# Third and fifth layer of an eight-layer kernel: output transposes and output projection of a group moved to the next round of the loop

## The chip, the cores and the metric

The kernel runs on one core of a Trainium2 chip. The metric is the device time of one execution in microseconds (us), compared by the median over runs. The engines are PE (TensorE; PEld are its weight loads), DVE (VectorE), ACT (ScalarE), POOL (GpSimd) and SP (SyncE, which here only issues DMAs). Each engine works through its own instructions in the order in which the program gives them, and waits at semaphores for the others.

## The reference

Eight residual layers are applied to x, of shape 128 sequences by 64 tokens by 128 features, in float32. Odd layers (first, third, fifth, seventh) are cross-attention to `ctx`; even ones are feed-forward layers. Only the third and the fifth are rearranged by the change:

```python
# third layer, "l1x": 16 heads of 8 features
q = (LN(x) @ Wq.T + bq) * scale;  k = ctx @ Wk.T + bk;  v = ctx @ Wv.T + bv
probs = softmax(q k^T + mask);    x = x + tanh(g) * ((probs v) @ Wo.T + bo)
# fifth layer, "l2x": 4 query heads of 32 features, one key/value head, rotary positions
q = rope(rms(LN(x)) @ q_w);  k = rope(rms(ctx) @ k_w);  v = rms(ctx) @ v_w
x = x + tanh(g) * (softmax(mask(q k^T)) v @ out_w)
```

## The kernel before, in words

x stays in SBUF for the whole kernel. Each layer walks over 32 groups of 256 tokens (four sequences; two tiles, t = 0 and 1, of 128 tokens). A layer is software-pipelined: `make_layers` (L126 to L150) gives it a string of items, and every engine passes the same string once per round (`traverse`, L491 to L521). A word's suffix is its lag against the round: `+` is the group after the round's own, `++` two after, `-` the group before, `--` two before. Each engine has its own `do`, which issues only what that engine has to do for an item, and nothing where it has no part. So an item's place in the string is its place in the queue of every engine that takes part in it.

```python
last = min(lag for _, lag in layer.order)
first = 1 if last >= -1 else 3
for i in range(-2, first):  iteration(...)           # written out
count = (NG - 2 - first) // 2                        # loop of two rounds each
for i in range(first + 2 * count, NG - last):        # written out
```

The items of the third and fifth layer, with the lines of their instructions:

- L: statistics of x (and of ctx in the fifth), nine to fifteen short DVE instructions (L1417 to L1450), then a power on POOL (L745) and on SP one DMA of the group's ctx (L595, L588).
- M: normalisation on DVE (L1458, L1462). F: transposes of the result on PE (L821, L825), copied out by ACT (L1200, L1194).
- QK (third): the query and key products on PE (L844 to L845), copied out by ACT (L1210, L1212), after which SP spreads the keys over the heads with 16 DMAs (L602). Q, K (fifth): products on PE, rotary arithmetic on DVE (L1619 to L1629). V: products on PE, copied out by ACT (L1225, L1233).
- S0, S1: scores of a tile on PE; then, in the same item, the DVE part of the softmax: mask, maximum, difference (L1540, L1543, L1545). In the third layer S0 waits on PE for all key-spreading DMAs of its group. P0, P1: the exponentials on ACT (L1260).
- T0, T1: transposes of the probabilities on PE (L942), copied out by ACT (L1266). The third layer has eight chunks, so each T takes two PSUM banks; the fifth has two chunks and takes one.
- A0, A1: probabilities times values on PE, then on DVE the reciprocal of the sums and the scaling into `o_sb` (L1663, L1667).
- X0, X1: transposes of `o_sb` on PE (L974), copied into `oT` by ACT (L1281, L1284). They wait until DVE has written `o_sb`.
- W0, W1: output projection on PE (L994); then on DVE, in the third layer, the bias (L1703) and the residual (L1578), in the fifth the residual alone. The last reader frees the PSUM bank: L1703 in the third layer, L1578 in the fifth.

T, A, X and W of one group share two PSUM banks, 6 and 7, in turn (`body_ring`): in the third layer T0 takes 6 and 7, T1 takes 6 and 7, A0 6, A1 7, X0 6, X1 7, W0 6, W1 7; in the fifth T0 6, T1 7, A0 6, A1 7, X0 6, X1 7, W0 6, W1 7. F, Q, K, V take banks 4 and 5, and the scores banks 0 to 3. Before PE writes a bank it waits until the bank's earlier content was read:

```python
def take(ring, g, u):                                    # L767
    b = ring.bank(g, u)
    pe.wait_ge(drained[b], ring.count(g, u) - 1)
    return b
```

The order of a ring's uses comes from the order of the string (L104 to L107).

Of the kernel before, what the change touches and what calls it, by code (L numbers as in the profile page):

```python
# [86 lines left out]
class Layer:  # L87
# [8 lines left out]
    def __init__(self, n, name, order, uses, body_banks, heads=0, scale=1.0, cross=False,  # L96
                 experts=0, top=0):
        self.n, self.name, self.order, self.uses = n, name, order, uses
        self.body_banks = body_banks
        self.heads, self.scale, self.cross = heads, scale, cross  # L100
        self.experts, self.top = experts, top
        self.front = []
        self.body = []
        for item, lag in order:  # L104
            if item[0] in ("L", "M", "H", "S", "P", "N"):
                continue
            (self.front if lag == 1 else self.body).extend([item] * uses.get(item[0], 1))  # L107
# [6 lines left out]
def stages(text):  # L114

    out = []
    for word in text.split():
        name = word.rstrip("+-")
        lag = word.count("+") - word.count("-")
        kind = name.rstrip("0123456789.")  # L120
        numbers = [int(k) for k in name[len(kind):].split(".")] if name != kind else [0]
        out.append(((kind, *numbers), lag))
    return out


def make_layers():  # L126
    attention = {"T": 2, "A": 2}
    narrow = {"T": 2, "A": 1}
    l0x = Layer(0, "l0x", stages(
        "L++ T0- S0 T1- S1 P0 F+ A0- M++ Q0+ N0 K0+ A1- N1 Q1+ P1 Q2+ W0- Q3+ W1- V0+"),  # L130
        attention, (6, 7), 16, 64 ** -0.5, True)
    l0f = Layer(1, "l0f", stages(
        "T1- S0 F+ T0- QK+ L++ G+ S1 A0- P0 H+ P1 E0.0+ E0.1+ A1- C+ V0+ N0 N1 Z0+ E1.0+ E1.1+ M++ Z1+"),
        narrow, (6, 7), 16, 8 ** -0.5, False, E_FF0, 2)
    l1x = Layer(2, "l1x", stages(
        "F+ S0 QK+ S1 L++ T0- T1- N0 A0- A1- P0 P1 N1 M++ V+ X0- X1- W0- W1-"),
        narrow, (6, 7), 16, 8 ** -0.5, True)
    l1f = Layer(3, "l1f", stages(
        "U0.0 U0.1 U0.2 L++ U1.0 U1.1 F+ D0 U1.2 U2.0 U2.1 U2.2 D1 U3.0 U3.1 D2 U3.2 "
        "U4.0 U4.1 U4.2 M++ D3 G+ D4 U5.0 U5.1 U5.2 H+ U6.0 U6.1 U6.2 D5 U7.0 U7.1 U7.2 "  # L140
        "D6 D7"), {}, (0, 1, 2, 3), experts=E_FF1, top=2)
    l2x = Layer(4, "l2x", stages(
        "S0 L++ F+ S1 Q+ T0- T1- P0 A0- P1 A1- K+ N0 M++ X0- X1- N1 W0- V+ W1-"),
        {"T": 1, "A": 1}, (6, 7), 4, 32 ** -0.5, True)
    l2f = Layer(5, "l2f", [], {}, (0, 1, 2, 3), experts=E_FF2, top=1)
    l3x = Layer(6, "l3x", stages(
        "T0- S0 T1- F+ P0 S1 Q2+ N0 Q0+ A0- K2+ P1 Q1+ A1- V2+ N1 K0+ W0- Q3+ K3+ L++ V0+ W1- M++ V3+ K1+ V1+"),
        attention, (6, 7), 16, 64 ** -0.5, True)
    l3f = Layer(7, "l3f", stages("KF L++ F+ M++ RF VF"), {}, (0, 1, 2))
    return [l0x, l0f, l1x, l1f, l2x, l2f, l3x, l3f]  # L150
# [73 lines left out]

def build(nc, x_in, ctx_in, ctxT_in, mask1_in, mask2_in, small_in, late_in, w1_in, w2_in, out):
    layers = make_layers()
    L0X, L0F, L1X, L1F, L2X, L2F, L3X, L3F = layers

# [1811 lines left out]
```

## Time and profile before

| | us |
|---|---|
| median of 3 runs | 4499.69 |
| lowest, highest | 4495.56, 4502.85 |
| the profiled execution, its own time | 4495.28 |
| its span, first to last instruction | 4493.3 |
| granted TensorE clock, mean over the span | 0.863 |

The rows further down are read like this. A row of the timeline is the start (us from the span's start), the length of a run of like instructions, the engine, the line and the operation, the tiles written and read, the count, and in brackets the engine's idle time just ahead and what ended it. In a row of stretches the columns are the stretch, its length, then for each engine its busy time with the count of instructions, the granted TensorE clock (1.00 is 2.4 GHz, 0.50 is 1.2 GHz), the DMA share and GB/s. The third layer runs from about 1374 to 1924 us, the fifth from about 2887 to 3262 us.

### The profile page before, as it was taken

To read this page: it belongs to the slowest core of one execution; us is meant where nothing else is said; L and a number is where in the kernel's file an instruction comes from. 1 tells how busy PE (TensorE), PEld (TensorE's weight loads), DVE (VectorE), ACT (ScalarE), POOL (GpSimd) and SP (SyncE) were. 2 spreads that over 40 slices of the span, in tenths; PEclk is the share of its full clock that TensorE was granted. 3 is DMA by queue.
4 is the path that set the end of the run, shared out by engine and by line. 5 is a ranking of instruction groups with operands and counts; after the bars stand their busy time and mean duration, and the time that the engine had idled before them with its cause. 6 is when DMAs were issued, how large, how long until landed. Compare 5 with 4: busy or idle time off the path is not lost.

```text
span 4493.3 us, 111186 instructions
## 1 busy us (share of the span) xinstructions
PE 3848.1 (86%) x38938; PEld 3008.1 (67%) x38938; DVE 2983.7 (66%) x9018; ACT 1953.3 (43%) x5436; POOL 884.4 (20%) x639
## 2 busy tenths in 40 slices
PE   5999978888886888889999999877845899999965
PEld 4777745555554556589999999755545767777754
DVE  4666657777765777766666666699972266666669
ACT  3666645655552434333333333222212355555521
POOL 1222223333330000010111111100062032222211
PEclk9999977777776767789999999988757999999976
DMA  3000010000001000000000000100004400000000
GB/s 130 8 7 8 7 23 6 6 6 6 6 7 68 15 16 15 14 6 0 0 0 0 0 0 3 43 11 11 8 22 166 147 13 12 12 12 12 10 13 26
DMA packets 102378, 98.15 MB, mean 22 GB/s; under 512 B 31728, under 2 KB 91120, under 8 KB 101616
## 3 DMA queue, kind: packets, MB, share of 16 engines
q1 hardware_dynamic: 97728, 77.99, 5.8%
q0 software_dynamic: 4096, 8.40, 0.6%
q10 hardware_dynamic: 432, 10.19, 0.6%
q8 instruction: 70, 1.15, 0.1%
q14 instruction: 52, 0.43, 0.0%
HBM read 48.02 MB, written 19.66 MB: 15 GB/s over the span
## 4 chain that ended last, share of the span: by engine, by line
PE 56%; DVE 20%; SPq 8%; issue 8%; POOL 3%; DMA 2%; ACT 2%; DVEq 1%; POOLq 0%; ACTq 0%
PE ps L781 52%; SPq L602 7%; PE ps L942 4%; DVE acc L1685 2%; DMA arena_a<-kT 1%; POOL route L753 1%; POOL scr L731 1%; DVE mx L1554 1%; DVE probs L1556 1%; DVE arena_b L1627 1%; DVE st L1417 1%; DVE o_sb L1667 1%; DVE xn L1458 1%; DVE vsmall L1635 1%; DVE mx L1543 1%
## 5 line engine op out<-in xcount | busy, mean ns | idle before, releaser
L781 PE MATMUL ps<-xcT,small 128*128 128x256 f32 x2176 | 618.4, 422 | 54.1 <-DMA xcT<-in_ctxT 27.2
L781 PEld LDWEIGHTS ps<-xcT,small 128*128 128x128 f32 x2176 | 412.4, 204 | 266.9 <-issue 105.5
L1294 ACT ACTIVATE kT<-ps 128x256 f32<-128x256 f32 (+1 forms) x768 | 294.4, 383 | 625.2 <-PE ps L781 549.0
L781 PE MATMUL ps<-arena_b,qT 64*64 64x64 f32 (+3 forms) x11136 | 543.6, 242 | 21.8 <-DVE arena_b L1627 20.4
L745 POOL TENSOR_TENSOR rstd<-veps,neghalf 128x2 f32<-128x2 f32 (+1 forms) x224 | 167.6, 748 | 1959.5 <-DVE veps L1450 1626.1
L759 POOL TENSOR_TENSOR probs<-probs,den 128x1024 f32<-128x1024 f32 x192 | 363.6, 1901 | 936.7 <-DVE den L1574 669.7
L781 PE MATMUL ps<-xhi,parts_a 128*128 128x256 f32 (+1 forms) x2112 | 501.2, 289 | 22.7 <-DVE qT L1714 22.7
L781 PE MATMUL ps<-small,xcT 128*64 128x64 f32 (+5 forms) x3072 | 482.1, 383 | 44.9 <-DVE acc L1685 33.1
L781 PEld LDWEIGHTS ps<-arena_b,qT 64*64 64x64 f32 (+3 forms) x11136 | 463.6, 149 | 59.1 <-issue 36.4
L1266 ACT ACTIVATE pT<-ps 128x512 f32<-128x512 f32 (+1 forms) x576 | 302.1, 571 | 435.6 <-PE ps L942 434.6
L1714 DVE TENSOR_TENSOR qT<-kT,ps 128x256 f32<-128x256 f32 (+1 forms) x768 | 316.5, 419 | 191.3 <-ACT kT L1294 184.0
L781 PE MATMUL ps<-xlo,parts_a 128*128 128x256 f32 (+1 forms) x1536 | 431.0, 281 | 0.0
L781 PEld LDWEIGHTS ps<-xhi,parts_a 128*128 128x128 f32 (+1 forms) x2112 | 350.1, 181 | 28.9 <-DVE qT L1714 28.0
L781 PE MATMUL ps<-small,oT 128*64 128x128 f32 (+1 forms) x2304 | 331.4, 295 | 22.4 <-ACT oT L1281 16.8
L942 PE MATMUL ps<-small,probs 128*128 128x128 f32 x2176 | 326.9, 296 | 17.4 <-ACT pT L1266 8.2
L781 PEld LDWEIGHTS ps<-small,oT 128*64 128x64 f32 (+1 forms) x2304 | 283.8, 155 | 83.3 <-issue 47.0
L942 PEld LDWEIGHTS ps<-small,probs 128*128 128x128 f32 x2176 | 262.6, 152 | 113.3 <-issue 81.5
L781 PEld LDWEIGHTS ps<-small,xcT 128*64 128x64 f32 (+1 forms) x3072 | 230.9, 180 | 154.5 <-DVE acc L1685 45.7
L781 PEld LDWEIGHTS ps<-vsmall,pT 128*128 128x128 f32 x2304 | 278.6, 197 | 71.6 <-issue 42.4
L781 PE MATMUL ps<-arena_a,qT 64*64 64x512 f32 (+1 forms) x1648 | 273.0, 633 | 45.9 <-DMA arena_a<-kT 45.9
L1274 ACT ACTIVATE oT<-ps 64x512 f32<-64x512 f32 x512 | 288.5, 587 | 48.5 <-PE ps L781 45.5
L1248 ACT ACTIVATE probs<-ps,negmax 128x64 f32<-128x64 f32 x1024 | 303.8, 418 | 0.0
(217 smaller groups left out, 7133.3 us busy)
## 6 DMA issues: line engine op xcount, KB each, us to landing
wbuf<-parts_b SPq DMA_DIRECT2D x39, 512.0 KB, 3.0
arena_a<-kT SPq DMA_DIRECT2D x1024, 8.0 KB
xcT<-in_ctxT SPq DMA_DIRECT2D x96, 128.0 KB, 2.1
xn<-scr SPq DMA_DIRECT2D x39, 128.0 KB, 2.2
scr_y<-acc SPq DMA_DIRECT2D x39, 128.0 KB, 2.9
scr<-vsmall SPq DMA_DIRECT2D x9, 512.0 KB, 13.4
ctx_sb<-in_ctx SPq DMA_DIRECT2D x32, 128.0 KB, 2.1
arena_a<-in_w ACTq DMA_DIRECT2D x1, 4096.0 KB, 12.1
```

The lines of the kernel that those rows point to most:

```text
L602: sp.dma_start(k_spread(g.par)[8 * h:8 * h + 8, h, :], kT[8 * h:8 * h + 8, g.par, :]).then_inc(s_kspread.sem(g), 16)
L731: pool.indirect_dma_start(out=scr[:, :], out_offset=bass.IndirectOffsetOnAxis(ap=place[:, t:t + 1], axis=0), in_=xn_all[:, t, :], in_offse ...
L745: pool.tensor_tensor(rstd[:, 0:n], veps[:, 0:n], neghalf[:, 0:n], ALU.pow).then_inc(s_rstd.sem, 1)
L759: pool.tensor_tensor(pr, pr, rv[:, t, 0:nh].unsqueeze(2).to_broadcast([P, nh, S]), ALU.mult).then_inc(s_probs.sem, 1)
L781: return nc.tensor.matmul(o, lhsT, rhs, start=start, stop=stop, skip_group_check=True)
L942: last = nc.tensor.transpose(bank(b)[:, i * P:(i + 1) * P], probs[:, g.par, t, c * P:(c + 1) * P], ident)
L1248: last = nc.scalar.activation(probs[:, g.par, t, h * S:(h + 1) * S], score_bank(b)[:, h * S:(h + 1) * S], ACT.Exp, bias=negmax[:, t, h:h + ...
L1266: nc.scalar.activation(pT[:, t, 4 * j:4 * j + n, :].rearrange("p c t -> p (c t)"), bank(b, n * P), ACT.Copy).then_inc(drained[b], 1)
L1274: last = nc.scalar.activation(oT[rows, t, :, hb * S:(hb + 1) * S], bank(b)[rows, :].rearrange("p (c q) -> p c q", q=S), ACT.Copy)
L1294: nc.scalar.activation(silu_buf(k)[0:n, :], bank(b)[0:n, 0:GT], ACT.Silu).then_inc(s_act.sem, 1)
L1685: add = dve.scalar_tensor_tensor(out=a, in0=src, scalar=cw, in1=a, op0=ALU.mult, op1=ALU.add)
L1714: dve.tensor_tensor(qT[0:n, e % 2, c, :], silu_buf(k)[0:n, :], bank(b)[0:n, GT:2 * GT], ALU.mult).then_inc(drained[b], 1)
```

## The change

In the third layer X0, X1, W0 and W1, which stood at the end of the round for the group before the round's own, now stand near its beginning for the group two before: it is the same group, reached one round later. X0 and X1 are put between F and S0, W0 between QK and S1, and W1 behind L. In the fifth layer X0 and X1 are put behind S0, and W0 and W1 behind F, ahead of S1. The sort in `Layer.__init__` only sees to it that the uses of banks 6 and 7 keep their order T, A, X, W. As the smallest lag is now -2, these two layers write out five rounds ahead of the loop in place of three and go one round further at the end.

```diff
-        for item, lag in order:
+        for item, lag in sorted(order, key=lambda e: -min(e[1], 0)):
...
     l1x = Layer(2, "l1x", stages(
-        "F+ S0 QK+ S1 L++ T0- T1- N0 A0- A1- P0 P1 N1 M++ V+ X0- X1- W0- W1-"),
+        "F+ X0-- X1-- S0 QK+ W0-- S1 L++ W1-- T0- T1- N0 A0- A1- P0 P1 N1 M++ V+"),
...
     l2x = Layer(4, "l2x", stages(
-        "S0 L++ F+ S1 Q+ T0- T1- P0 A0- P1 A1- K+ N0 M++ X0- X1- N1 W0- V+ W1-"),
+        "S0 X0-- X1-- L++ F+ W0-- W1-- S1 Q+ T0- T1- P0 A0- P1 A1- K+ N0 M++ N1 V+"),
```

## Rows read from the trace of the kernel before

**Rows 1.** Source view of L1545 in the third, then in the fifth layer (one per tile)
```profile
L1545 DVE TENSOR_TENSOR probs<-probs,mx x64: 1224/1224/1227, 1379.0 to 1907.1; 128x1024 f32<-128x1024 f32 x64
...
L1545 DVE TENSOR_TENSOR probs<-probs,mx x64: 424/424/426, 2895.7 to 3254.0; 128x256 f32<-128x256 f32 x64
```

**Rows 2.** Stretches: the steady part of the third layer, then of the fifth
```profile
1417.00:1900.00 483.00, 424.71 (x2635) 278.89 (x2638) 346.68 (x796) 193.19 (x370) 19.49 (x28) 0.70 0.06 16
2890.00:3250.00 360.00, 285.44 (x1676) 185.59 (x1674) 337.83 (x1254) 97.91 (x277) 30.20 (x30) 0.80 0.04 11
```

**Rows 3.** Chain that ended last, third layer, 1600 to 1634 us: start, length, what
```profile
1599.70 0.67 SPq L602
...
1609.09 0.62 SPq L602
...
1609.75 1.81 DMA arena_a<-kT
1611.56 0.14 issue
1611.69 4.00 PE ps L781 x12
```

**Rows 4.** Timeline of the third layer, one round and the start of the next
```profile
1611.69 1.99 PE L781 MATMUL ps<-arena_a,qT 64*64 64x512 f32 x8 [1.03 <-DMA arena_a<-kT]
...
1614.00 1.22 DVE L1540 SCALAR_TENSOR_TENSOR probs<-masked,ps 128x1024 f32<-128x1024 f32 x1 [2.63 <-PE ps L781]
...
1616.51 1.22 DVE L1545 TENSOR_TENSOR probs<-probs,mx 128x1024 f32<-128x1024 f32 x1
1616.59 10.67 SPq L602 DMA_DIRECT2D arena_a<-kT  x16
...
1617.53 1.14 PE L942 MATMUL ps<-small,probs 128*128 128x128 f32 x8
1617.94 1.22 DVE L1540 SCALAR_TENSOR_TENSOR probs<-masked,ps 128x1024 f32<-128x1024 f32 x1 [0.21 <-issue]
...
1620.26 3.76 PE L781 MATMUL ps<-vsmall,pT 128*128 128x36 f32 x32 [0.20 <-ACT pT L1266]
...
1621.60 0.48 DVE L1417 BATCH_NORM_STATS2 st<-x_sb 128x6 f32 x2
...
1623.07 0.36 DVE L1663 RECIPROCAL den<-ps 128x32 f32<-128x32 f32 x1
...
1625.10 0.60 DVE L1458 TENSOR_SCALAR xn<-x_sb,mv,rstd 128x128 f32 x2
...
1626.80 0.29 DVE L1703 TENSOR_TENSOR acc<-ps,small 128x128 f32<-128x128 f32 x1 [1.10 <-PE ps L781]
...
1626.98 0.63 PE L821 MATMUL ps<-small,xn 128*128 128x128 f32 x2
1627.26 0.35 DVE L1578 SCALAR_TENSOR_TENSOR x_sb<-acc,tgate,x_sb 128x128 f32 x1 [0.17 <-DVE acc L1703]
```

**Rows 5.** Stretches of that round, third layer: transposes to values, then the rest
```profile
1617.60:1624.30 6.70, 6.25 (x60) 5.66 (x62) 6.24 (x18) 4.18 (x6) 0.69 (x1) 1.00 0.05 12
1624.50:1633.40 8.90, 7.45 (x31) 3.42 (x28) 4.78 (x10) 2.50 (x7) 0.00 (x0) 0.50 0.07 20
```

**Rows 6.** Timeline of the third layer's last transposes and value products
```profile
1912.11 3.26 PE L942 MATMUL ps<-small,probs 128*128 128x128 f32 x16
...
1915.63 4.82 PE L781 MATMUL ps<-vsmall,pT 128*128 128x36 f32 x32 [0.26 <-issue]
```

**Rows 7.** Stretches beside rows 6: clock while transposing, then in the values' first half
```profile
1911.30:1914.60 3.30, 3.05 (x13) 2.78 (x14) 1.28 (x4) 1.25 (x3) 0.00 (x0) 0.50 0.00 0
1915.70:1917.90 2.20, 2.20 (x21) 2.20 (x21) 0.28 (x1) 0.32 (x1) 0.00 (x0) 1.00 0.00 0
```

**Rows 8.** Timeline of the fifth layer, from one score product to the next
```profile
3061.23 0.20 DVE L1663 RECIPROCAL den<-ps 128x8 f32<-128x8 f32 x1
...
3065.49 1.12 PE L781 MATMUL ps<-arena_b,qT 128*64 128x256 f32 x4 [0.75 <-DVE arena_b L1627]
...
3066.38 0.60 DVE L1578 SCALAR_TENSOR_TENSOR x_sb<-ps,tgate,x_sb 128x128 f32 x2
...
3067.03 0.42 DVE L1540 SCALAR_TENSOR_TENSOR probs<-masked,ps 128x256 f32<-128x256 f32 x1
...
3070.51 1.06 PE L942 MATMUL ps<-small,probs 128*128 128x128 f32 x4
...
3071.71 1.15 PE L781 MATMUL ps<-vsmall,pT 128*128 128x132 f32 x8
...
3072.91 0.20 DVE L1663 RECIPROCAL den<-ps 128x8 f32<-128x8 f32 x1
```

**Rows 9.** Waits of PE in the fifth layer, 2890 to 3250 us: total, times, longest
```profile
PE ps L974 <- DVE o_sb L1667: 43.0, 54, 2.2
```

## The prediction

> **What bounds the kernel now.** I read the source view of L1545 first, because it gives the rounds: 64 instructions, two per group, so 32 groups and 31 steps from group to group. In the third layer they span 528.1 us [rows 1]; the last comes one tile (3.94 us) after its group's first, so a round is (528.1 - 3.9)/31 = 16.9 us. In the fifth it is (358.3 - 3.5)/31 = 11.45 us. The stretches tell what is full in them. In the third layer nothing is: DVE is busy 347 of 483 us, 72%, and PE's 425 us hold waits and slow clock (0.70). In the fifth DVE is busy 338 of 360 us, 94% [rows 2].
>
> The chain shows what closes the third layer's round: 16 DMA issues on SP from 1599.70 to 1609.71, a landing of 1.81, PE's scores and products for 4.00, ACT's copies for 0.9, and SP starts again at 1616.59 [rows 3, 4]. That is a loop through SP, PE and ACT. DVE has a gap of 2.63 us in it, PE one of 1.03. The fifth layer is a DVE queue; PE waits 43 us in X for `o_sb` there [rows 9], which costs nothing while DVE is full.
>
> **Part 1, the third layer on PE and SP.** No instruction is added or taken away. X0 and X1 go into the PE gap ahead of S0, W0 behind QK, W1 behind S1. QK stays directly behind S0, so keys reach SP as early as now; SP and POOL have no part in X and W, and L stays behind QK on SP. By this alone the loop of rows 3 stays at 16.9 us: worth nothing.
>
> **Part 2, the third layer on DVE: the new wait.** Bank 7 is freed by L1703 of W1. Before, DVE did that at the end of the round (1627.5), and the next T0 came later. Now DVE has W1 behind the softmax of S0, W0, the softmax of S1 and the statistics, and T0 follows W1 on PE and takes bank 6 and then bank 7. T0's second half must wait for DVE to reach W1. Behind it in PE's queue stand T1, A0, A1, V, F, X0, X1 and S0. F waits for M, which stands behind A1 on DVE; X1 waits for A1's `o_sb`; and the next S0 stands behind both. So the round closes through DVE and PE one after the other. From PE's start of S0, with the durations of rows 4:
>
> - to DVE's first softmax instruction: 1614.00 - 1611.69 = 2.31
> - softmax of S0: 1616.51 + 1.22 - 1614.00 = 3.73
> - W0 on DVE: L1703 and L1578, about 0.72 (0.29, 0.17 of wait, 0.35, partly laid together)
> - softmax of S1: 1621.60 - 1617.94 = 3.66. Its scores are there in time, just: PE needs 1.99 for S0, 2.0 for QK, 0.5 for W0, 1.99 for S1 and 0.3 to show, 6.8 against DVE's 6.76
> - statistics: 1623.07 - 1621.60 = 1.47
> - bias of W1, which frees bank 7: 0.29. Sum so far 12.2; PE has stood idle from about 7.8 on
> - T0's second half and T1, until A starts. Now four banks take 1620.26 - 1617.53 = 2.73; without the first one 2.2
> - A0 and A1: 3.76
> - end of A (1624.02) to the end of M (1625.70): 1.68
> - F's second transpose, X0, X1 and the start of S0: four transposes, F's two taking 0.63: 0.9
>
> Together 12.2 + 2.2 + 3.76 + 1.68 + 0.9 = 20.7 us, against 16.9. SP's loop, still 16.9 long, is covered then.
>
> **The clock in it.** T and A run at clock 1.00 today, and everything after them at 0.50 [rows 5]. The clock rises at the end of the dense S0, QK, S1 and falls 6.8 us later, by the end of A, although PE issued without a pause. After the change PE has about 4.5 us with no matmul between S1 and T0's second half. The clock that S1 won is then lost before A begins, as I see it. A at half clock has one case in the trace: 32 products took 4.82 us [rows 6], of which 21 began in the first 2.2 us at 1.00 [rows 7] and the other 11 took some 2.4 us, 0.22 each. All 32 at half clock: 7.0 in place of 3.76. Transposes at half clock took 3.5 us to the start of A for four banks [rows 6, 7], so 2.65 for three in place of 2.2. The round is then 12.2 + 2.65 + 7.0 + 1.68 + 0.9 = 24.4 us. In that one case the clock had risen during dense transposes at 0.50; I allow one round in five for that, with half of A's surcharge of 3.2 saved, and take 24.1.
>
> Rule against rule: the Trainium skill (TensorE: Matmul & The Clock Gate, Part 1, on oscillation) says that pauses between groups of matmuls, also those made by cycling PSUM banks, throttle the clock again so that each next burst starts slow. It speaks against this change; by it A runs at half clock in every round (24.4 us). No row of before has a pause ahead of A, so none shows it.
>
> **Third layer:** 31 x (24.1 - 16.9) = +223 us. Ends: 31 x (20.7 - 16.9) = +118, and 31 x 7.5 = +233, some more if a term of the sum is short.
>
> **Part 3, the fifth layer.** W0 and W1 are freed by DVE ahead of S1 here, so T0 waits for one short softmax and the statistics only. DVE's work is the same 10.9 us a round. What changes is when PE is ready. First, S0 starts when the keys are rotated (3065.49), and DVE has 0.9 us of M left and, now, 0.6 of residual before it turns to the scores at 3067.03 [rows 8]. With the residual gone it is there at 3066.4; the scores at half clock (1.12 and about 0.2 to show) come at 3066.8: 0.4 lost, nothing at full clock. Second, PE has X, F and W ahead of S1, Q and T. A's products start 4.68 us after DVE's softmax (3071.71) and DVE needs the first of them 5.88 after it (3072.91); X and W put 1.3 us in front at half clock, and DVE starts its round 0.65 earlier relative to PE, while its own need moves back 0.65 by W: 0 to 1.2 us lost. Together 0 to 1.6; I take 0.9, as the clock is at 0.80 on average and not at half throughout. 31 x 0.9 = +28 us; ends -20 (DVE's whole idle time of 22 us over 360 vanishing with PE's waits of rows 9) and +50.
>
> **Part 4, the ends of the layers.** Three rounds less in the loops (two, and one more at the end) and longer written-out parts: the same instructions per group. The last W comes directly behind X there, as no softmax is left in between. I cost it at nothing; ends -3 and +5. Other layers keep their order, since the sort moves nothing with lag -1 to 2.
>
> **Sum.** 223 + 28 = +251. On the profiled execution's own 4495.3 (span 4493.3 and 2 around it) this is 4746; that execution lies 4.4 below the median shown, 4499.7, so 4751 on the median. A difference within 0.2%, 9 us, is what a measurement of this kernel can't tell from none.
>
> **Rivals.**
> - A keeps its clock. For: T and A begin at 1.00 in each round now, and in rows 6 and 7 it rose again during the transposes. Against: the pause. Then 118 + 28: 4646. Chance 0.20.
> - Longer still: the scores of S0 or S1 come later than summed, or the fifth layer loses 1.6 a round and the key DMAs meet the statistics: 4500 + 245 + 50 = 4795. Chance 0.09.
> - Not slower. The place is T0's second bank in the third layer. The wait decides only when the loop through DVE is longer than SP's 16.9; if it were 3.8 us shorter than my 20.7 (bank 7 freed by 8.4 instead of 12.2 us after S0), the third layer stays as it is, by part 1, and the fifth may give up its 20 us: 4480 to 4500. For: parts 1 and 3, and that the busy share of DVE in the third layer is only 72%. Against: 3.8 us is one whole tile of softmax, and its place ahead of W1 is plain in the string. Chance 0.08: faster 0.04, same 0.03.
> - The change does nothing it says (the sort undone, or bank order kept otherwise): the string alone decides, so this has no room; 0.01 in same.
>
> **How the numbers follow.** My forecast, half clock in A, has 0.63 and gives the predicted time. The range goes from just below the first rival (118 in the third layer with nothing lost in the fifth is 4618; I cut at 4630) to 4800. Outside it lie the not-slower cases and little of either end. Slower by over 0.2% takes all but 0.08: 0.92.
>
> **What would show it.** Right: the spacing of L1545 in the third layer near 24 us (21 if the clock holds); PE idle 4 to 5 us ahead of L942, released by DVE L1703; no DMA wait ahead of S0; the clock 0.50 in the A stretch, 32 products over 7 us. In the fifth: L974 no longer waits for `o_sb`, and DVE waits appear ahead of L1540 and L1663. Wrong: spacing still 16.9 with SP closing the chain, or T0's second bank released by something else than L1703.

## The result, and the profile after

| us | before | after |
|---|---|---|
| median of 4 runs | 4501.27 | 4718.13 |
| lowest, highest | 4495.56, 4504.62 | 4714.6, 4720.15 |
| the profiled execution, its own time | 4495.28 | 4720.15 |
| its span | 4493.3 | 4718.3 |
| granted TensorE clock, mean | 0.863 | 0.850 |

The ratio is 1.048, with a 95% interval of 1.046 to 1.050: slower by 217 us where 251 were forecast. The time lies inside the range, 33 us below the number given.

The source view of L1545 after, third and then fifth layer, beside [rows 1]:

```profile
L1545 DVE TENSOR_TENSOR probs<-probs,mx x64: 1224/1224/1227, 1381.8 to 2112.0; 128x1024 f32<-128x1024 f32 x64
...
L1545 DVE TENSOR_TENSOR probs<-probs,mx x64: 424/424/426, 3111.0 to 3478.2; 128x256 f32<-128x256 f32 x64
```

The span of the profiled execution grew by 225.0 us, 8 us more than the medians did. From these rows and [rows 1] it divides so: up to the first softmax of the third layer +2.8, in which the changed rounds have no part; the third layer's rounds 730.2 against 528.1, +202.1; from its last L1545 to the first of the fifth 999.0 against 988.6, +10.4; the fifth layer 367.2 against 358.3, +8.9; the rest +0.8. The third layer holds nine tenths of it. With 4.2 us between the last two tiles, a round there takes (730.2 - 4.2)/31 = 23.4 us against 16.9.

What ends the waits of the third layer, 1417 to 2100 us (total, times, longest):

```profile
DVE den L1663 <- PE ps L781: 224.4, 57, 6.0
PE ps L942 <- DVE acc L1703: 176.2, 58, 5.4
...
DVE probs L1540 <- PE ps L781: 89.5, 28, 3.3
```

PE now stands 176 us ahead of the transposes (L942) for the bias (L1703), as forecast. What this wait brings with it is larger still: DVE stands 224 us for the value products, which start late and mostly run slow, against 2.2 us in this layer before. No DMA ends a wait of PE in this stretch any more, so SP's loop is covered.

One round of the third layer, timeline, beside [rows 4]:

```profile
1699.78 1.99 PE L781 MATMUL ps<-arena_a,qT 64*64 64x512 f32 x8
...
1702.09 1.22 DVE L1540 SCALAR_TENSOR_TENSOR probs<-masked,ps 128x1024 f32<-128x1024 f32 x1 [3.19 <-PE ps L781]
...
1704.60 1.23 DVE L1545 TENSOR_TENSOR probs<-probs,mx 128x1024 f32<-128x1024 f32 x1
1705.74 0.28 DVE L1703 TENSOR_TENSOR acc<-ps,small 128x128 f32<-128x128 f32 x1
1706.08 0.66 PE L942 MATMUL ps<-small,probs 128*128 128x128 f32 x4 [1.36 <-DVE acc L1703]
...
1706.50 1.22 DVE L1540 SCALAR_TENSOR_TENSOR probs<-masked,ps 128x1024 f32<-128x1024 f32 x1
...
1710.15 0.48 DVE L1417 BATCH_NORM_STATS2 st<-x_sb 128x6 f32 x2
...
1711.60 0.28 DVE L1703 TENSOR_TENSOR acc<-ps,small 128x128 f32<-128x128 f32 x1
...
1711.94 2.92 PE L942 MATMUL ps<-small,probs 128*128 128x128 f32 x12 [5.21 <-DVE acc L1703]
...
1714.65 6.98 PE L781 MATMUL ps<-vsmall,pT 128*128 128x36 f32 x32
...
1721.67 0.36 DVE L1663 RECIPROCAL den<-ps 128x32 f32<-128x32 f32 x1 [2.43 <-PE ps L781]
...
1724.18 1.99 PE L781 MATMUL ps<-arena_a,qT 64*64 64x512 f32 x8
...
1736.41 2.92 PE L942 MATMUL ps<-small,probs 128*128 128x128 f32 x12 [5.23 <-DVE acc L1703]
...
1739.12 4.02 PE L781 MATMUL ps<-vsmall,pT 128*128 128x36 f32 x32
```

The second half of T starts 12.16 us after S0 (12.2 in the sum), 5.21 us after PE last worked. The round is 1724.18 - 1699.78 = 24.40 us. In the next one the clock rose while A ran: A took 4.02 in place of 6.98, and the round is short by that much. Over the layer 30 A stand behind such a wait; 25 of them took about 7.0 us and five took 4.0 to 4.3.

Stretches of the same two rounds: up to the wait, the wait, the transposes behind it, A, and A of the next round (length, busy time and count of PE, weight loads, DVE, ACT and POOL, then the granted clock, DMA share, GB/s):

```profile
1702.80:1706.70 3.90, 2.54 (x18) 1.19 (x16) 3.67 (x6) 0.84 (x2) 0.00 (x0) 1.00 0.02 6
1706.80:1711.90 5.10, 0.00 (x0) 0.00 (x0) 4.92 (x14) 0.57 (x1) 0.04 (x1) 0.72 0.05 11
1711.90:1714.60 2.70, 2.66 (x12) 2.29 (x13) 0.35 (x1) 1.20 (x2) 0.66 (x1) 0.50 0.05 12
...
1714.70:1721.50 6.80, 6.80 (x33) 6.79 (x32) 0.94 (x3) 2.49 (x3) 0.00 (x0) 0.50 0.07 21
1739.20:1742.40 3.20, 3.20 (x28) 3.20 (x28) 0.93 (x3) 2.49 (x3) 0.00 (x0) 0.91 0.15 44
```

The clock is full before the wait, falls within it while PE has no matmul at all, and stays at half through T and A. This is the step on which the forecast and the first rival parted.

### The profile page after: what moved, and what is told of

Same layout as the page of the kernel before. It is cut to its first block, busy times and chain, and to the rows that moved or that the text cites. A ratio compares the mean times of both kernels' runs of the same rounds, so it can differ in the third digit from the quotient of the medians.

```text
span 4718.3 us, 110993 instructions
## 1 busy us (share of the span) xinstructions
PE 3904.0 (83%) x38938; PEld 3107.0 (66%) x38938; DVE 2985.9 (63%) x9018; ACT 1950.5 (41%) x5436; POOL 885.0 (19%) x639
## 4 chain that ended last, share of the span: by engine, by line
PE 60%; DVE 24%; issue 9%; POOL 3%; SPq 2%; ACT 1%; DVEq 1%; DMA 1%; POOLq 0%; ACTq 0%
PE ps L781 52%; PE ps L942 5%; DVE mx L1543 2%; DVE probs L1540 2%; DVE acc L1685 2%; POOL route L753 1%; PE ps L821 1%; POOL scr L731 1%; DVE st L1417 1%; DVE mx L1554 1%; DVE probs L1556 1%; DVE arena_b L1627 1%; DVE xn L1458 1%; DVE o_sb L1667 1%; SPq L602 1%
## 5 line engine op out<-in xcount | busy, mean ns | idle before, releaser
L781 PE MATMUL ps<-xcT,small 128*128 128x256 f32 x2176 | 606.8, 417 | 52.3 <-DMA xcT<-in_ctxT 26.8
L942 PE MATMUL ps<-small,probs 128*128 128x128 f32 x2176 | 363.3, 318 | 195.1 <-DVE acc L1703 182.0
L942 PEld LDWEIGHTS ps<-small,probs 128*128 128x128 f32 x2176 | 286.2, 163 | 269.2 <-DVE acc L1703 189.0
L781 PEld LDWEIGHTS ps<-vsmall,pT 128*128 128x128 f32 x2304 | 358.9, 245 | 62.0 <-issue 43.3
L781 PE MATMUL ps<-vsmall,pT 128*128 128x32 f32 (+2 forms) x2304 | 368.5, 326 | 10.5 <-ACT pT L1266 9.9
L781 PE MATMUL ps<-small,oT 128*64 128x128 f32 (+1 forms) x2304 | 321.3, 290 | 6.1 <-ACT oT L1274 5.5
```

The lines of the kernel that those rows point to most:

```text
L781: return nc.tensor.matmul(o, lhsT, rhs, start=start, stop=stop, skip_group_check=True)
L942: last = nc.tensor.transpose(bank(b)[:, i * P:(i + 1) * P], probs[:, g.par, t, c * P:(c + 1) * P], ident)
```

## The experiments

Each ratio is against the kernel before, run on the same chip beside it (medians 4496.8 to 4498.5 us). The first five are edits of the changed kernel, and their diffs start from it, as is the split with the change's third layer further down; the others are edits of the kernel before. All that keep the third layer's X and W a round later, other than the change itself, have the fifth layer's string of before. The diffs show only the lines that matter; runs with a moved X and W have the sort of the change too.

**Each layer alone.** First the third layer's string of the change, the fifth as before:

```diff
-        "S0 X0-- X1-- L++ F+ W0-- W1-- S1 Q+ T0- T1- P0 A0- P1 A1- K+ N0 M++ N1 V+"),
+        "S0 L++ F+ S1 Q+ T0- T1- P0 A0- P1 A1- K+ N0 M++ X0- X1- N1 W0- V+ W1-"),
```

> Third layer as in the change, fifth as before. Bank theory (T0 waits for DVE's bias add of W1, which frees bank 7): nearly the whole loss is here. Rounds of the third layer 24.4 us where the value products run at half clock, 21.5 where they keep some full clock, and about +211 us in all: 4712. Rival (both layers pay for the written-out rounds and for the later X and W alike): about half of the loss, 4610.

Measured: 4708.21 us, ratio 1.046 (1.045 to 1.048), nearly the whole loss. Then the fifth layer's string of the change, the third as before:

```diff
-        "F+ X0-- X1-- S0 QK+ W0-- S1 L++ W1-- T0- T1- N0 A0- A1- P0 P1 N1 M++ V+"),
+        "F+ S0 QK+ S1 L++ T0- T1- N0 A0- A1- P0 P1 N1 M++ V+ X0- X1- W0- W1-"),
```

> Fifth layer as in the change, third as before. Bank theory: rounds 11.85 us in place of 11.6, since DVE waits for the scores of S0 and no longer has the residual to do meanwhile; +9 to +12 us in all: 4512. Rival (both layers pay alike): 4600.

Measured: 4504.96 us, ratio 1.0015 (1.0005 to 1.0024), some 7 us, less than the 9 to 12 expected. The two make 1.048 together, the ratio of the whole change: the parts add up.

**Where W1 stands in the third layer.** It was moved ahead of S1, so that its bias no longer stands behind the second softmax:

```diff
-        "F+ X0-- X1-- S0 QK+ W0-- S1 L++ W1-- T0- T1- N0 A0- A1- P0 P1 N1 M++ V+"),
+        "F+ X0-- X1-- S0 QK+ W0-- W1-- S1 L++ T0- T1- N0 A0- A1- P0 P1 N1 M++ V+"),
```

> Third layer as in the change, but W1 directly behind W0, ahead of S1; fifth as before. X and W stay a round later. Bank theory: DVE frees bank 7 at about 7.5 us after S0 starts instead of 12.2, PE has just ended S1, the value products keep the full clock, the loop through DVE is 16.2 us and SP's loop of 16.9 closes the round again: spacing 16.9, time 4500 to 4512 (the end of the layer may keep its 9 us). Rival (it is the place of X ahead of S0 and of W behind QK on PE that costs, or the later round itself): spacing 20 or more, over 4600.

Measured: 4502.53 us, ratio 1.0006 (0.9997 to 1.0016): no difference. X and W still stand a round later and still share their banks with T; only the place of one item in the queues is another, and the whole loss is gone. PE and DVE in its timeline:

```profile
1614.92 1.98 PE L781 MATMUL ps<-arena_a,qT 64*64 64x512 f32 x8 [0.76 <-DMA arena_a<-kT]
...
1620.87 0.28 DVE L1703 TENSOR_TENSOR acc<-ps,small 128x128 f32<-128x128 f32 x1
...
1621.21 2.72 PE L942 MATMUL ps<-small,probs 128*128 128x128 f32 x16 [0.25 <-DVE acc L1703]
1621.59 0.28 DVE L1703 TENSOR_TENSOR acc<-ps,small 128x128 f32<-128x128 f32 x1
...
1623.90 4.29 PE L781 MATMUL ps<-vsmall,pT 128*128 128x36 f32 x32
...
1631.80 1.98 PE L781 MATMUL ps<-arena_a,qT 64*64 64x512 f32 x8 [0.74 <-DMA arena_a<-kT]
```

The bias of W1 is done at 1621.87, about when PE comes to the second half of T; the only wait for a bias in this round is 0.25 us, and S0 waits for the keys again, in a round of 16.88 us. This is part 1 of the prediction shown by itself: the later round costs nothing and gives nothing while SP's loop sets the pace.

Halfway between, W1 was put behind S1 but ahead of the statistics (L):

```diff
-        "F+ X0-- X1-- S0 QK+ W0-- S1 L++ W1-- T0- T1- N0 A0- A1- P0 P1 N1 M++ V+"),
+        "F+ X0-- X1-- S0 QK+ W0-- S1 W1-- L++ T0- T1- N0 A0- A1- P0 P1 N1 M++ V+"),
```

> Third layer as in the change, but W1 ahead of L: behind S1's softmax and before the statistics; fifth as before. Bank theory: bank 7 is freed 1.47 us earlier in each round, so 22.9 us where the products run at half clock and 20.0 where they do not, 31 x 1.4 = 45 us less than with the third layer's change alone: about 4667. Rival (W's place on DVE is without effect as long as it stays behind S1): 4712.

Measured: 4645.17 us, ratio 1.032 (1.030 to 1.034), with rounds of 21.55 us in the mean, 1.7 less than with the third layer's change alone (23.3), and so 22 us below the time expected. A round in which A runs at half clock takes 23.0 and not 24.4: that 1.4 is the statistics. The other 0.3 of a round comes from more rounds at the full clock, which was not expected. Three transposes and value products in a row of that kernel's timeline:

```profile
1738.24 2.92 PE L942 MATMUL ps<-small,probs 128*128 128x128 f32 x12 [3.78 <-DVE acc L1703]
1740.95 6.99 PE L781 MATMUL ps<-vsmall,pT 128*128 128x36 f32 x32
...
1761.20 2.82 PE L942 MATMUL ps<-small,probs 128*128 128x128 f32 x12 [3.76 <-DVE acc L1703]
1763.81 4.17 PE L781 MATMUL ps<-vsmall,pT 128*128 128x36 f32 x32
...
1781.30 2.46 PE L942 MATMUL ps<-small,probs 128*128 128x128 f32 x12 [3.78 <-DVE acc L1703]
1783.56 6.99 PE L781 MATMUL ps<-vsmall,pT 128*128 128x36 f32 x32
```

The same pause of 3.8 us comes before an A of 6.99 and one of 4.17. The granted clock was 0.90 in the first of these pauses and 1.00 in the other two; in the transposes behind them it was 0.50, 0.53 and 0.62. So here the clock could also fall behind the pause, and the length of the pause alone does not settle what A costs; the rounds get shorter either way.

**The clock apart from the wait.** The changed third layer was kept, with its wait, and PE was given matmuls to do in it: 13 products of one projection's weights behind W1 (26 matmuls in the trace), into a score bank that is overwritten before anyone reads it. They compute nothing that the output uses.

```diff
+                    if layer is L1X and t == 1 and not (type(g.pair) is int and 2 * g.pair + g.par + 2 >= NG):
+                        scores = layer.score_ring
+                        pe.wait_ge(drained[scores.bank(g.ahead(2), 0)], scores.count(g.ahead(2), 0))
+                        for _ in range(13):
+                            mm(ps[:, scores.bank(g.ahead(2), 0), 0:GT], w("l1x_wq"), xcT[:, g.par, 0:GT])
```

> Third layer's change alone, and 13 more products of 128x256 on PE behind W1, written to the score banks of tile 0 that DVE has already read (their result is used by nothing); PE works through its pause with them, the waits stay as they are. Clock theory (the pause loses the clock, and the value products then run at half of it): the clock stays 1.00 to the end of the value products in every round, rounds of 20.7 us instead of 24.4, 4708 - 24 x 3.7 - 6 x 0.9 = about 4614. Rival (the clock falls there for another reason, or the extra work delays the transposes): 24.4 and 4708 as before, or longer.

Measured: 4604.3 us, ratio 1.024 (1.022 to 1.025). That is 104 us faster than the same kernel without the extra work (4708.21; the kernel before stood at 4498.5 and 4498.3 in the two comparisons). The timeline of PE and its weight loads in one round (this kernel's L1708 is L1703 of the others), and the stretch 1420 to 1850 us:

```profile
1695.45 1.99 PE L781 MATMUL ps<-arena_a,qT 64*64 64x512 f32 x8
...
1701.38 5.78 PE L781 MATMUL ps<-xcT,small 128*128 128x256 f32 x26
1706.99 2.62 PE L942 MATMUL ps<-small,probs 128*128 128x128 f32 x16
...
1707.61 0.42 PEld L942 LDWEIGHTS ps<-small,probs 128*128 128x128 f32 x4 [0.26 <-DVE acc L1708]
...
1709.62 3.76 PE L781 MATMUL ps<-vsmall,pT 128*128 128x36 f32 x32
...
1715.93 1.99 PE L781 MATMUL ps<-arena_a,qT 64*64 64x512 f32 x8
```

```profile
1420.00:1850.00 430.00, 405.81 (x2465) 297.98 (x2465) 255.42 (x581) 140.43 (x271) 13.92 (x20) 0.84 0.05 13
```

The same stretch of the kernel without them:

```profile
1420.00:1850.00 430.00, 312.33 (x1656) 235.49 (x1656) 218.42 (x504) 121.89 (x234) 12.52 (x18) 0.65 0.04 11
```

5.8 us of useless products fill the pause, A takes 3.76, the clock of the stretch is 0.84 against 0.65, and the steady round is 20.4 to 20.5 us: about the 20.7 that the sum gives with A and T at full clock. In four of the layer's earlier rounds A still took 4.1 to 4.9, so "in every round" was too much to expect. The bias of W1 still stands behind the second softmax in DVE's queue, and the second half of T still starts behind it, 12.16 us after S0 (1707.61 against 1695.45), as without the products. What went is the clock's part: from there to A 2.01 us in place of 2.71, and A 3.76 in place of 6.98, some 3.9 us in a round. The loss of 210 us with the third layer alone is thus about half the wait (106 us left) and half the clock (104). The second half comes only with the first: with W1 ahead of S1 both are gone.

**The other limit: SP's loop.** In the kernel before, 8 of the 16 key DMAs of a group were issued from POOL's queue, and PE and ACT wait for both halves (the lines of these waits and of the semaphore are left out here):

```diff
-                    for h in range(16):
+                    for h in range(16 if layer is L0F else 8):
...
+                if item == ("QK", 0) and layer is L1X:
+                    pool.wait_ge(drained[layer.front_ring.bank(g, 1)], layer.front_ring.count(g, 1))
+                    pool.sem_inc(s_ready, 1)
+                    for h in range(8, 16):
+                        pool.dma_start(k_spread(g.par)[8 * h:8 * h + 8, h, :],
+                                       kT[8 * h:8 * h + 8, g.par, :]).then_inc(s_khalf[g.par], 16)
```

> Order of the kernel before; in the third layer 8 of the 16 key-spreading DMAs are issued by POOL instead of SP. If SP's loop closes the third layer's rounds in the kernel before (16.9 us), and POOL needs no longer for 8 than SP for 8, S0 starts right behind F's transposes, about 0.95 us earlier: rounds of 16.0, 4498 - 29 = 4470. If POOL needs over 1.2 us for each DMA, its 8 close the loop: 16.9 or more. Rival (DVE or PE closes the rounds, and the DMA wait is only what is left over): no change.

Measured: 4456.72 us, ratio 0.991 (0.989 to 0.992), 42 us faster than before, with rounds of 15.6 us. Rows of its timeline (its lines stand a few further down):

```profile
1607.21 0.68 PE L828 MATMUL ps<-small,xn 128*128 128x128 f32 x2
1607.83 1.98 PE L788 MATMUL ps<-arena_a,qT 64*64 64x512 f32 x8
...
1612.59 5.36 SPq L603 DMA_DIRECT2D arena_a<-kT  x8
...
1616.06 4.14 POOL L744 DMA_DIRECT2D arena_a<-kT  x8 [11.69 <-issue]
```

S0 stands directly behind F, with no wait for keys. So the issuing closed the old round, as the chain of [rows 3] said, and it was worth 1.3 us a round where 0.95 were expected. What is next is no single engine: the chain of 1590 to 1625 us runs half through PE's products (L788, 50.6%) and for 14% through DVE's mask and maximum (L1551, L1554). Why the round fell below the 16.0 expected wasn't looked into. The Trainium skill (DMA: Bandwidth & Descriptors, Rules for kernel authors) says that spreading DMAs over several engines only saves the issue time of a queue. The rows show that saving, SP's issues taking 5.36 us in place of 10.67, and here that time was what the round waited for; whether bandwidth gains, no run here shows.

The same split with the harmless order, W1 ahead of S1:

> The split of the key-spreading DMAs between SP and POOL together with the order X0, X1 a round later ahead of S0, W0 and W1 behind QK and ahead of S1. The loop through DVE and PE, 16.2 us by the wait of 0.75 us that is left ahead of S0, closes the round: 31 x 0.75 = 23 us off, 4478. If the order had something to give that SP's loop hid, it would show here as less than the kernel before with the same split.

Measured: 4473.74 us, ratio 0.994 (0.993 to 0.996). With SP's loop out of the way the later round for X and W is the worse order, by 17 us, of which 12 lie between the first and the last L1545 of the third layer (498.7 us against 486.8); before, that loop hid it. And the split with the change's third layer:

> Third layer in the order of the change with its key-spreading DMAs shared between SP and POOL, fifth as before. Bank theory: the loop through DVE and PE closes these rounds and SP's loop of 16.9 us lies inside them, so the split that took 42 us off the kernel before takes nothing off here: rounds of 24.4 and 21.5, 4708. Rival (SP still closes the rounds, its DMAs only start later): some 40 us less, 4666.

Measured: 4701.65 us, ratio 1.045 (1.043 to 1.047). Of the 42 us that the split gave to the kernel before some 6 are left, within the intervals of the two. Only the first two rounds are clearly shorter (12.8 and 14.6 us, against 17.3 and 16.8 with the third layer's change alone); they have no W of an earlier group yet and so no wait on L1703. From 1417 to 2100 us no wait of PE ends with a DMA, so SP isn't what closes the other rounds.

**The fifth layer with a full front.** X and W were put ahead of S0 in the kernel before, the third layer left as it was:

```diff
-        "S0 L++ F+ S1 Q+ T0- T1- P0 A0- P1 A1- K+ N0 M++ X0- X1- N1 W0- V+ W1-"),
+        "X0-- X1-- W0-- W1-- S0 L++ F+ S1 Q+ T0- T1- P0 A0- P1 A1- K+ N0 M++ N1 V+"),
```

> Third layer as before; fifth with X0, X1, W0, W1 of two rounds back at the very front, ahead of S0. The fifth layer lost time, by the theory, because DVE no longer had the residual to do while S0's scores came, and because W stood ahead of Q on PE. Here DVE's order is that of the kernel before again, and PE does X and W while it waits for the keys: rounds 11.5 as before, time 4498, or up to 6 us less where PE's clock gains. Rival (one round later costs by itself): 4505 as with the fifth layer's change alone.

Measured: 4494.74 us, ratio 0.9989 (0.998 to 0.9999): about 4 us by the medians, hardly to be told from none. So the later round by itself costs the fifth layer nothing; the rival's 4505 is out. A gain isn't shown by the trace either. Its L1545 rows span 353.6 us in the fifth layer, but it is the fastest execution of the ten (4486.27); kernels with the fifth layer of before span 355.5 to 358.3, and the next one, with the same new string, 356.2. Put together with the split:

> Third layer in the order of before with its key-spreading DMAs shared between SP and POOL, fifth layer with X and W of two rounds back at the very front. The two gains lie in different layers and bounds, so they add: 4457 - 4 = 4453, third layer 15.6 us a round, fifth 11.4.

Measured: 4452.28 us, ratio 0.991 (0.989 to 0.992), the lowest median of all, but not to be told from the split alone. The split is the gain that is shown.

## Why the prediction was right, and where it was off

**Part 1, the later round by itself.** Right. With W1 out of the second softmax's way the time is that of before, and S0 waits for DMA again.

**Part 2, the wait.** Right, term by term, in the round shown above: to the softmax 2.31 (2.31 forecast); the first softmax 3.74 (3.73); the second 3.65 (3.66); statistics 1.45 (1.47); the second half of T 12.16 after S0 (12.2); T to A 2.71 (2.65); A 6.98 (7.0); end of A to the next S0 2.55 (1.68 + 0.9). The sum is 24.40 us, the number of the working. Moving one item ahead of one softmax takes it all away, and moving it ahead of the statistics takes 1.4 us, their length, off a round with A at half clock. One reading was off without effect: PE had ended its work ahead of the wait 6.96 us after S0 started and not 7.8, since what stands between S0 and the wait ran faster than summed (S1 took 1.09 us, not 1.99); so the pause is 5.2 us and not 4.5.

**The clock.** The mechanism was right: with PE idle the clock fell inside the pause, and A ran at half. The Trainium skill (TensorE: Matmul & The Clock Gate, Part 1) says that pauses between bursts of matmuls throttle the clock again, so that the next burst starts slow. This trace agrees for 25 of the 30 A behind the pause (about 7.0 us each) and not for the other five (4.0 to 4.3), and the experiment that fills the pause bears out that the pause is what costs the clock. What was mis-sized is the allowance for a risen clock, one round in five with half of A's surcharge saved. Five rounds were shortened by it, a smaller share, but they saved 2.8 each and not 1.6, as A's first products already met the rising clock: 14 us where 10 were allowed. The larger error was to count all 31 rounds as alike. The first two took 17.34 and 17.63: without an earlier group's W nothing held the second half of T back, and S0 waited for a DMA as before. That is 14 us less. The last took 21.5 with A at half clock, as it has no statistics and no F: 3 us less. 31 x 24.4 = 756.4, less 5 x 2.8, 13.8 and 2.9, is 725.7; measured, 726. So the third layer gave +202 for +223.

**Part 3, the fifth layer.** Half right. The first loss came as described:

```profile
3306.96 1.12 PE L781 MATMUL ps<-arena_b,qT 128*64 128x256 f32 x4 [3.07 <-DVE arena_b L1627]
...
3308.36 0.42 DVE L1540 SCALAR_TENSOR_TENSOR probs<-masked,ps 128x256 f32<-128x256 f32 x1 [0.44 <-PE ps L781]
...
3313.35 1.14 PE L781 MATMUL ps<-vsmall,pT 128*128 128x132 f32 x8 [0.24 <-ACT pT L1266]
...
3314.83 0.20 DVE L1663 RECIPROCAL den<-ps 128x8 f32<-128x8 f32 x1
...
3319.10 0.65 PE L781 MATMUL ps<-arena_b,qT 128*64 128x256 f32 x4 [3.16 <-DVE arena_b L1627]
...
3319.99 0.42 DVE L1540 SCALAR_TENSOR_TENSOR probs<-masked,ps 128x256 f32<-128x256 f32 x1
```

These are rows of the timeline of the fifth layer after. At half clock the scores take 1.12 and DVE loses 0.44; at full clock they take 0.65 and it loses nothing. What DVE waited for in the layer, 3120 to 3470 us:

```profile
DVE probs L1540 <- PE ps L781: 6.8, 18, 0.7
...
DVE den L1663 <- PE ps L781: 0.3, 1, 0.3
```

The first loss is 6.8 us in 18 rounds, most of the layer's +8.9. The second loss, products of A that come too late for DVE, did not come: in the round shown the first of them start at 3313.35, 1.48 us ahead of the reciprocal, and in the whole stretch DVE waits for A once, for 0.3 us. The term of 0 to 1.2 us was measured at 0. The 1.3 us that X and W were to put ahead of A are not there: A starts 4.99 us after DVE's first softmax instruction, 4.68 before. With +8.9 us over the layer, the 0.9 a round was 0.3: an error of 19 us, next to the third layer's 21. (The round of before was also read a little short, 11.45 us: the last tile there follows its group's first by 1.3 us and not 3.5, which gives 11.5. Nothing hangs on it.)

**Part 4, the ends.** It was costed at nothing, with ends of -3 and +5, and +10.4 came after the last softmax of the third layer, most of it in its tail. There two groups' value products stand behind it in place of one. Rows of the timeline:

```profile
2116.20 7.00 PE L781 MATMUL ps<-vsmall,pT 128*128 128x36 f32 x32
...
2129.58 4.56 PE L781 MATMUL ps<-vsmall,pT 128*128 128x36 f32 x32 [0.22 <-issue]
...
2137.48 0.79 ACT L1182 ACTIVATE parts_a<-small 128x704 fp32r<-128x704 f32 x1 [1.32 <-DVE acc L1703]
```

The next layer begins 25.5 us after the last L1545, against 16.7 before. That each group has the same instructions is true and was the wrong question: what counts is how many of them are left when the last softmax is done, and the change had put the A of the last group but one behind it, where it had run beside it. The further 2.8 us ahead of the third layer are no effect of the change. With the third layer's strings of before, and nothing else changed ahead of it, the first L1545 came at 1382.6 us in one trace and at 1373.8 in another.

**How the errors add.** In the trace the third layer gave 21 us less than forecast and the fifth 19 less, and 14 came that had no term (10.4, 2.8 and 0.8): 251 - 40 + 14 = 225. Another 8 us are that the medians differ by 217. The mechanism and the third layer's round were right. That the total is off by 34 us only, and not by the 40 of the two layers and more, is in part luck, since the ends were mis-sized the other way.

**The rivals.** A does not keep its clock through the pause; with the pause filled it does, and the time is then 4604 us, where this rival said 4646 with 28 of the fifth layer in it, 4618 without. So its price is about that of the wait without the clock. Longer still did not come either: PE had written the scores of S1 4.5 us after S0 started, ahead of DVE's need, and the fifth layer lost 0.3 us a round and not 1.6. Not slower was lost at its place, the second bank of T: bank 7 came free 12.16 us after S0 and not by 8.4.

## What to carry to other kernels

An item that is moved in a hand-written order is moved in every engine's queue at once; ask of each PSUM bank that it touches which instruction frees it, and what stands ahead of that instruction in its own queue. If a softmax stands there, all of TensorE waits through it. Price such a wait twice, once by its length and once by the clock at which the work behind it will run (here 106 and 104 us); and count the rounds in which the wait is really there, with the rounds that pile up behind the last one.

## What was not expected

- 5.8 us of useless products in each round made a kernel 104 us faster. The 32 value products behind them took 3.76 us in place of 6.98, 0.12 us each against 0.22.
- The same pause (3.8 us) was followed by an A of 6.99 and one of 4.17 us in neighbouring rounds. So the cost of a pause of that length varies from round to round; with one of 5.2 us A ran at half clock in 25 of 30. What decides it wasn't tried.
- Sixteen small DMA issues take SP 10.67 us and were what closed the round before. Eight of them on POOL took 4.14 us there beside SP's 5.36.
